# Row quantisation of the cross attention input: one of two VectorE passes replaced by a ScalarE pass, the lower clamp folded into ScalarE's Relu

## The reference

```
def fake_quant(x, scale, zp):
    q = jnp.clip(jnp.round(x / s + z), QMIN, QMAX)     # 0 and 255; z is 128
    return (q - z) * s
q1 = fake_quant(x1, x1_scale, x1_zp)
q2 = fake_quant(x2, x2_scale, x2_zp)
return jnp.matmul(q1, q2)
```

## Time and profile before

| what | value |
|---|---|
| median of 3 runs | 1863.63 us (1861.92 to 1865.05) |
| the profiled execution | 1863.91 us, its span in the trace 1862.1 us |
| PE busy | 1775.8 us (95%) |
| DVE busy | 1329.5 us (71%) |
| ACT busy | 970.2 us (52%) |
| POOL busy | 641.7 us (34%) |
| mean clock granted to PE | 0.992 |

### The profile page before, as it was taken

The page is one execution under the profiler, slowest core; times in us unless marked ns, Lnnn a source line. Parts: engine busy times, 40 slices in busy tenths (PEclk is TensorE's granted clock), DMA queues, the critical chain, the costliest instruction groups (busy, mean ns, idle before and its releaser), DMA issues.

```text
span 1862.1 us, 27416 instructions
## 1 busy us (share of the span) xinstructions
PE 1775.8 (95%) x9865; PEld 893.7 (48%) x9865; DVE 1329.5 (71%) x1867; ACT 970.2 (52%) x1432; POOL 641.7 (34%) x506
## 2 busy tenths in 40 slices
PE   6999999999999999999999999999999999999887
PEld 4454545444454545445454545445454545574333
DVE  7667776767677776767777766667677766659877
ACT  5555454645455454655454444555454444534674
POOL 2352334324342334324333333424333332301433
PEclk9999999999999999999999999999999999999998
DMA  4223224241423224241422214131322214133332
GB/s 172 84 69 108 69 90 108 72 105 46 136 63 108 69 91 108 69 107 46 136 63 69 74 57 108 57 85 46 98 67 68 75 57 108 57 106 122 114 91 91
DMA packets 158116, 161.52 MB, mean 87 GB/s; under 512 B 99872, under 2 KB 127904, under 8 KB 157600
## 3 DMA queue, kind: packets, MB, share of 16 engines
q1 hardware_dynamic: 146528, 147.09, 27.0%
q0 software_dynamic: 2560, 8.39, 1.4%
q10 hardware_dynamic: 8896, 4.28, 0.8%
HBM read 123.56 MB, written 12.58 MB: 73 GB/s over the span
## 4 chain that ended last, share of the span: by engine, by line
PE 67%; DVE 15%; issue 9%; ACT 7%; POOL 1%; DMA 1%; ACTq 0%; DVEq 0%; POOLq 0%
PE bank L1391 16%; PE bank L1393 16%; PE bank L1392 16%; PE bank L1364 4%; PE bank L1478 4%; PE bank L1480 4%; PE bank L1479 4%; DVE w_pair L1743 2%; DVE gated_split L1743 2%; DVE acc L1912 1%; DVE bank L1852 1%; PE bank L1542 1%; PE bank L1553 1%; DVE k_units L1892 1%; ACT L1632 1%
## 5 line engine op out<-in xcount | busy, mean ns | idle before, releaser
L1391 PE MATMUL bank<-x_blocks,w_pair 128*128 128x512 f16 (+1 forms) x1820 | 678.3, 373 | 34.4 <-ACT gate_units L1632 22.9
L1392 PE MATMUL bank<-x_blocks,w_pair 128*128 128x512 f16 (+1 forms) x1820 | 677.9, 372 | 0.0
L1393 PE MATMUL bank<-x_blocks,w_pair 128*128 128x512 f16 (+1 forms) x1820 | 677.9, 372 | 0.0
L1391 PEld LDWEIGHTS bank<-x_blocks,w_pair 128*128 128x128 f16 x1820 | 177.9, 98 | 241.2 <-ACT gate_units L1632 29.8
L2030 POOL TENSOR_TENSOR sums_pair<-raw_pair 128x512 f32<-128x512 f32 x63 | 92.4, 1467 | 563.8 <-DVE w_pair L1743 409.6
L1393 PEld LDWEIGHTS bank<-x_blocks,w_pair 128*128 128x128 f16 x1820 | 178.0, 98 | 202.8
L1392 PEld LDWEIGHTS bank<-x_blocks,w_pair 128*128 128x128 f16 x1820 | 178.1, 98 | 188.6
L1912 DVE TENSOR_TENSOR acc<-acc,bank 128x512 f32<-128x512 f32 x320 | 211.3, 681 | 20.8 <-PE bank L1480 20.5
L1641 ACT ACTIVATE bank<-bank 128x512 f32<-128x512 f32 x145 | 84.7, 584 | 211.1 <-PE bank L1393 210.9
L2056 POOL TENSOR_TENSOR ssq<-ssq,sig 128x512 f32<-128x512 f32 x64 | 81.8, 1278 | 283.8 <-ACT sig L1662 283.8
L1743 DVE SCALAR_TENSOR_TENSOR w_pair<-raw_pair,w_pair 128x1024 f16<-128x1024 f32 x126 | 158.8, 1270 | 21.2 <-ACT w_pair L1606 21.1
(11 more groups left out here) (216 smaller groups left out, 2677.4 us busy)
## 6 DMA issues: line engine op xcount, KB each, us to landing
raw_pair<-w_qk SPq DMA_DIRECT2D x32, 1024.0 KB, 5.5
raw_pair<-w_gate SPq DMA_DIRECT2D x16, 1024.0 KB, 4.9
raw_pair<-w_out SPq DMA_DIRECT2D x16, 1024.0 KB, 4.9
raw_pair<-w_vt SPq DMA_DIRECT2D x15, 1024.0 KB, 5.0
raw_pair<-ctx_in SPq DMA_DIRECT2D x8, 1024.0 KB, 4.9
decay_sb<-rates SPq DMA_DIRECT2D x60, 128.0 KB, 4.5
acc<-x_t SPq DMA_DIRECT2D x4, 1024.0 KB, 11.4
ctx<-raw_pair SPq DMA_DIRECT2D x8, 512.0 KB, 3.0
```

What stands on the lines that cost most here:

```text
L1391: pe.matmul(out, w_hi, x_hi, start=unmet and k == 0, stop=False, skip_group_check=halves or not fresh)
L1392: pe.matmul(out, w_hi, x_lo, start=False, stop=False, skip_group_check=halves or not fresh)
L1393: mm = pe.matmul(out, w_lo, x_hi, start=False, stop=k == QT - 1, skip_group_check=halves or not fresh)
```

## The change

`quantise` now takes three passes in another division. ACT's first pass uses Relu in place of Identity, so that the lower clamp to 0 is done by it. DVE makes one pass instead of two: minimum with 255, then plus the rounding constant, in place in fp32. A second, new ACT pass (Identity with scale 1 and a bias of minus the constant and minus 128, read from a one-column buffer `unround`) takes the constant off and writes the bf16 result. That pass waits for `q1_clamped`, for the constants, and for its destination to be free, and it is written directly behind the first one. DVE sets `unround` with one more small memset beside those of L1751 and L1752.

```
         self.ones32, self.neg_half = late[:, 0:P], late[:, P:P + ST]
+        self.unround = late[:, P + ST:P + ST + 1]
...
         elif kind == "quantise":
...
-            act.activation(c.raw[st["slot"]][:, :], c.acc[b][:, st["s"], :], ACT.Identity, bias=c.z1,
+            act.activation(c.raw[st["slot"]][:, :], c.acc[b][:, st["s"], :], ACT.Relu, bias=c.z1,
                            scale=c.inv1).then_inc(sem["q1_scaled"])
+            act.wait_ge(sem["constants"], 1)
+            act.wait_ge(sem["q1_clamped"], st["clamped"][1])
+            until(act, sem, st["dst_free"])
+            act.activation(c.q1_n[b][st["s"] % 2][:, :], c.raw[st["slot"]][:, :], ACT.Identity, bias=c.unround,
+                           scale=1.0).then_inc(sem["q1_n"])
...
             dve.memset(c.neg_half, -0.5)
+            dve.memset(c.unround, -(ROUND + Q_MID))
             dve.memset(c.ones32, 1.0).then_inc(sem["constants"])
...
         elif kind == "quantise":
             src = c.raw[st["slot"]][:, :]
             dve.wait_ge(sem["q1_scaled"], st["scaled"][1])
-            dve.tensor_scalar(src, src, 0.0, Q_MAX, ALU.max, ALU.min).then_inc(sem["q1_clamped"])
-            dve.wait_ge(sem["q1_clamped"], st["clamped"][1])
-            until(dve, sem, st["dst_free"])
-            dve.tensor_scalar(c.q1_n[b][st["s"] % 2][:, :], src, ROUND, ROUND + Q_MID, ALU.add,
-                              ALU.subtract).then_inc(sem["q1_n"])
+            dve.tensor_scalar(src, src, Q_MAX, ROUND, ALU.min, ALU.add).then_inc(sem["q1_clamped"])
```

## The result

The changed kernel takes **1869.51 us** (median of 6 runs, 1868.32 to 1870.93), the kernel before on the same chip 1863.53 (6 runs). The ratio is 1.0034, with a 95% interval of 1.0024 to 1.0045: 6.0 us more, where 6.4 were forecast. The profiled execution of the changed kernel took 1868.32 us, span 1866.3, and is the shortest of its six.

The account below looks back on a forecast made before the run. The prediction took DVE as full in the early tiles and PE as near full from 1760, with ACT's in-order queue deciding the cost. Tile terms summed to 6.40 us on the 1863.63 median, giving 1870.0 us, range 1865.5 to 1872.5.

Parts of the forecast that it names:

- T3: Third of eight row tiles: the square stands behind ACT's new pass, so DVE's gating comes later, +1.05 us.
- T5: Fifth row tile: two copies for batch 0's last store stand behind the new pass, delaying issue and first gather, +1.66 us.
- T7: Seventh row tile: Gelus and a split stand directly behind the new pass, and DVE's next split waits, +1.94 us.
- T6: Sixth row tile: up-weight split moves 1.94 us, covered by DVE's 1.80 us idle for POOL: 0, bounds -0.5 to +0.3.
- T1 and T2: First two row tiles: 0.44 us gained at first, then Silu late behind the new pass and DVE waits, +1.25 us.
- T4: Fourth row tile: quantised rows 0.44 us later for PE, less 0.38 slack before the store's transposes, +0.06 us.
- T8: Last row tile: PE, already waiting 0.68 us for the quantised rows, gets them 0.44 later, +0.44 us.
- The new pass: Added ACT pass of 128x1024 at each tile: 1.13 us, between 1.05 and 1.24, holding ACT for 1.04.
- rival (b): Half is taken up: 2.3 us of early delays hidden before the gather, 1867.7 us, or 1866.7; chance 0.20.
- Rival (a): Offload works: shifts behind the new pass fall into idle time, DVE's saving leaves 1.9 us less, 1861.7; chance 0.09.
- Rival (c): PE's clock stays low longer after longer waits at T3 and T5, costing another 1 to 3 us, 1871 to 1873; chance 0.11.

Follow-up runs that it names:

- T5 alone: The change's new form at the fifth row tile only, the old form at the other seven, against the kernel before: 1863.35 us, ratio 1.0008.
- T7 alone: The change's new form at the seventh row tile only, the old form at the other seven, against the kernel before: 1864.27 us, ratio 1.0013.
- saving alone: Against the kernel before: Relu in ACT's first pass, one DVE pass, no second ACT pass, upper clamp left out: 1863.71 us, ratio 0.9982.
- second trace of the changed kernel: The changed kernel run again, unaltered, on another chip: 1870.31 us against 1866.81 for the kernel before, ratio 1.0017.
- before again: The kernel before, unchanged, run and traced as if it were a changed one: 1862.76 us, ratio 1.0001.
- changed (second, third): Two repeats of the unaltered changed kernel on two other chips: 1870.31 us, ratio 1.0017, and 1870.67 us, ratio 1.0044, against the kernel before.
- T1/T4/T6/T8: The change's new form at these four row tiles only, the old form at the other four, against the kernel before: 1863.42 us, ratio 0.9985.
- wait alone: The kernel before plus ACT's wait for DVE's clamp after its first pass, no second ACT pass, both DVE passes kept: 1867.74 us, ratio 1.0007.
- pass twice: The changed kernel plus a third ACT pass per tile, copying the raw buffer onto itself before the new pass: 1877.16 us, ratio 1.0054.
- T2/T3/T5/T7: The change's new form at these four row tiles only, the old form at the other four, against the kernel before: 1870.09 us, ratio 1.0021.
- deferred: The changed kernel with the new ACT pass and its wait some steps later in ACT's queue at five tiles: 1862.89 us, ratio 0.9981.
- clamp in the copy: Against the kernel before: lower clamp in ACT's first pass, upper clamp in its existing transpose copy, one DVE pass, none added: 1864.39 us, ratio 0.9987.

## Why the prediction came true, step by step

The mechanism holds, and the largest terms (T3, T5 up to the store's issue, T7) came as worked out. That the sum is right within 0.3 us is in part luck: up to the issue of the store the shift is 0.64 less than my terms give, it loses 0.64 more ahead of T6's clamp, and the pass at T6 costs 0.92 where I had put 0.

| step | forecast | shift in the changed trace | by an experiment |
|---|---|---|---|
| T1 and T2 | +1.25 | +1.06 (-0.63 and +1.69) | +1.68 with T1 in the old form |
| T3 | +1.05 | +1.10 | +1.11 with T1, T4, T6, T8 in the old form |
| between T3 and the next gating | 0 | -0.30 | -0.31 with only T5 or only T7 changed |
| T4 | +0.06 | -0.15 | not apart |
| T5 | +1.66 | +1.67 | +1.67 alone up to the issue, 2.55 up to T8 |
| T6 | 0 | +0.27 (-0.64 and +0.92) | +0.07 with T2, T3, T5, T7 in the old form |
| T7 | +1.94 | +2.01 | +1.95 alone |
| T8 | +0.44 | +0.45 | +0.50 with T2, T3, T5, T7 in the old form |
| sum | 6.40 | 6.11 | |

**The new pass.** Taken at 1.13 us, measured 1.147. It held ACT for 1.05 us (1690.44 to 1691.49). The Trainium skill (ScalarE: Activation LUTs, What ACT_TABLE_LOAD costs) gave the same 1.13 as an estimate. The trace agrees within 0.02.

**T1 and T2: right in kind, 0.19 too high.** I let T1 gain 0.44, the wait of PE that the earlier trace rows shows. It gained 0.63. PE no longer waits for its sum there:

```profile
1684.85 1.46 PE L1365 MATMUL bank<-x_blocks,gated_split 128*128 128x512 f16 x6
```

The key split of T2 waited 2.76 where I had said about 2.7.

**T3: right.** The gating waits for the square, for 1.75 us where I had said 1.6. PE waits less than I thought, 3.05 and not some 4 us.

**T3 to T4: a gain that I did not have.** 0.30 go between T3 and the next gating, in the changed trace and in those of T5 alone and T7 alone. Why is not shown.

**T4: a sign I could not have read off.** I charged 0.06 for the late quantised rows. By the shift, DVE's gain was 0.15 larger than its wait for PE. Ahead of the store (1736.03) PE now waits for nothing, where it had waited 0.38.

**T5: right to 0.01.** First pass at R = 1742.07, copies at R + 3.09 (forecast 3.02). The first gather comes 4.26 later (forecast about 4), so rival (b) is out: the gap between T3 and T5 does not take the delay. It takes 0.45 of the shift (2.16 at T3's gating, 1.71 at T5's first pass), of which 0.30 also goes in traces in which nothing ahead had changed. The 4.26 is right by luck, though: my terms up to the issue of the store sum to 4.02, and the issue came at 3.38; the gather then came 5.40 us behind the issue where it had come 4.52, which I had left as it was. Why it takes longer is not shown.

```profile
1751.66 1.22 POOL L2076 DMA_INDIRECT acc<-x_t,perm_sb  x1 [10.04 <-issue]
```

**T6: the term that was mis-sized.** I took 0 with a bound of +0.3, and 0.27 came, but as the rest of two larger amounts. Between the issue and T6's clamp the shift falls from 3.38 to 2.74: DVE had waited 0.77 there. Behind the clamp it rises to 3.66, so the new pass costs 0.92 and is not covered. The 1.80 us of idle time were no fixed cover. POOL's instruction that is under way when DVE's split of the up weights ends always ends shortly behind it. In before that is the second gather, which takes 2.84 us where it takes 0.96 in the changed kernel; DVE's split and that gather:

```profile
1749.34 2.29 DVE L1743 SCALAR_TENSOR_TENSOR w_pair<-w_pair 128x2048 f16<-128x2048 f32 x1 [0.38 <-ACT w_pair L1719]
1749.62 2.84 POOL L2073 DMA_INDIRECT acc<-x_t,perm_sb  x1 [0.30 <-issue]
```

In the changed kernel both gathers are over in time, and it is the first of the power operations, with 1.95 us where it had 0.26:

```profile
1753.74 2.29 DVE L1749 SCALAR_TENSOR_TENSOR w_pair<-w_pair 128x2048 f16<-128x2048 f32 x1 [3.06 <-ACT w_pair L1725]
1754.17 1.95 POOL L2067 TENSOR_SCALAR scores_keys<-scores_keys 128x1 f32<-128x1 f32 x1
```

It is so in all fourteen traces: a gather ends 0.82 to 1.09 us behind the split, a power operation 0.08 or 0.09. DVE's idle time behind the split is therefore 1.80, 0.78 or 0.00 us by which of POOL's instructions it is, and it moves with the split. In the kernel with T5 alone it is the first gather, the idle time is 3.32, and that is where its shift grows from 0.66 to 2.18. That DVE's split holds POOL up is my reading of these times; no run varies it.

**T7 and T8: right.** From ACT's first pass to the next Gelu it takes 3.14 us where I had 3.07; PE waits 1.37 for T8's rows where it had waited 0.68, and 0.68 + 0.44 beyond it is 1.12, so PE itself came a little earlier:

```profile
1781.76 0.62 PE L1506 MATMUL bank<-ident,gate_units 128*128 128x128 bf16 x8 [1.37 <-ACT gate_units L1705]
```

**Rival (a)** was wrong in its condition, and its price was too small. The Trainium skill (Perfetto Trace Analysis, Optimizing Scalar/DVE Operations) says that with a saturated VectorE it may make sense to move work to ScalarE. Here that holds only with a better place in ACT's queue: written directly behind the first pass it costs 6.11 us at T8, some steps later T8 comes 0.30 earlier. As for the price, I had summed DVE's saving to 1.9; the trace of the saving alone gives 3.4. I had left out that the rows come 0.7 earlier at T8, where the earlier trace rows shows PE waiting for them, and the 0.3 behind T3.

**Rival (c)**, a lower PE clock behind the longer waits, did happen in the first trace and cost nothing up to T8. Behind T3's transposes the product took 5.96 us, where before, with a shorter low stretch, it took 4.68:

```profile
1709.49 5.96 PE L1522 MATMUL bank<-x_blocks 128*128 128x512 bf16 x16
```

In the second trace of the changed kernel the granted clock is 1.00 in the windows around T3 and T7 (in the first it is 0.83 and 0.86), that product takes 3.61 us, and the shift at T8 is 6.11 all the same:

```profile
1700.00:1720.00 20.00, 14.89 (x102) 7.72 (x100) 16.66 (x31) 10.37 (x14) 3.34 (x6) 1.00 0.75 250
...
1760.00:1780.00 20.00, 17.28 (x115) 6.60 (x112) 15.73 (x29) 17.42 (x26) 6.73 (x9) 1.00 0.25 67
```

PE is not the last there, so its slower pieces lie beside the others' work. My premise that the clock is low after such a wait does not hold either: in the second trace PE waits 3.05 us at T3, and its transposes then take 0.61 us, at full clock.

## What to carry to other kernels

In this kernel a pass moved to an engine with idle time cost nothing only at a place in that engine's queue where nothing urgent stands behind it: look there, and not at the busy share. Count the wait for the other engine apart from the pass, since it holds up the same work even if the pass were free. Where an operation fits into a pass that is made anyway (here a clamp as Relu in a scaling and in a copy), it took 3.9 us off the shift at T8, and the added pass put 6.1 on it. Shifts of single tiles cannot simply be added: where another engine is waited for, the same pass cost 0.07 or 0.92 us at T6.

## What the runs showed of the hardware that I had not expected

**Clock in the tail.** Behind T8 the shifts of the traces part again, by up to 4 us between the last sums of the two batches (PE, 1807.91 and 1840.74 in before). That goes with PE's granted clock in the 4 us windows at that piece of work. In the trace of before, of the changed kernel, and of before again:

```profile
1808.00:1812.00 4.00, 4.00 (x26) 2.76 (x28) 1.87 (x9) 0.45 (x1) 1.38 (x2) 0.67 0.59 179
1812.00:1816.00 4.00, 4.00 (x26) 1.61 (x24) 2.75 (x7) 3.44 (x8) 0.84 (x1) 0.90 0.00 0
```

```profile
1812.00:1816.00 4.00, 2.66 (x24) 2.27 (x26) 2.49 (x7) 0.63 (x1) 2.65 (x3) 1.00 0.69 193
1816.00:1820.00 4.00, 4.00 (x32) 1.69 (x26) 3.09 (x11) 3.96 (x8) 1.04 (x1) 1.00 0.24 70
```

```profile
1808.00:1812.00 4.00, 4.00 (x21) 2.27 (x20) 1.44 (x8) 0.94 (x2) 1.08 (x2) 0.51 0.44 125
1812.00:1816.00 4.00, 4.00 (x20) 2.26 (x18) 2.35 (x6) 2.21 (x6) 0.34 (x1) 0.63 0.00 0
```

The last column but two is the granted clock, and 0.50 of it is the lower level, 1.2 GHz. In the 4 us ahead of these windows it is 1.00 in all three, with PE busy for 1.92, 2.81 and 2.36 us of the 4. What the clock falls short of 1.00, summed over the 4 us windows from 1804 to 1828, goes with the distance between the two products:

| short of full clock, summed | traces | distance against before |
|---|---|---|
| 0 | changed (first), T1/T4/T6/T8 | -1.59, -1.44 us |
| 0.42, 0.43 | before; changed (second, third), wait alone, pass twice, T2/T3/T5/T7 | -0.03 to +0.04 |
| 0.85, 0.86 | before again, deferred, T5 alone, T7 alone | +1.58 to +1.62 |
| 1.28 | saving alone, clamp in the copy | +2.63, +2.75 |

A difference of 0.43 of the full clock over 4 us is 1.7 us of matmuls at full clock, which is about what a step of the table shows. In the last row the low stretch begins about 1.1 us ahead of the first of the two products, so a part of it lies outside the distance. The same program has it one way or the other from one execution to the next (before and before again differ by 1.58 us in it), so a single trace says nothing on a change of 2 us at the end of the kernel. Why PE gets one or the other is not shown by any run.

**The kernel before differs by chip, the changed one does not.** Its median was 1863.5, 1866.3, 1866.8 and 1862.4 us in the four groups of runs, the changed kernel's 1869.5, 1870.3 and 1870.7. Why it was 3 to 4 us slower in two groups stays open: no trace of it was taken there, and the clock in the tail is a candidate only. The mean granted clock of each run is on record, and it does not explain it: the runs of the kernel before at 0.992 have medians of 1866.2 and 1866.4 us in the two groups and 1862.8 in the last. How much of the advantage that the deferred pass, the clamp in the copy and the four light tiles had there would show on another chip is therefore open too; by the traces it is 0.30, 3.88 and 1.26 us up to T8, the last with 0.74 of clock in it.

**Three prices of one ScalarE pass.** At 128x1024 it takes 1.06 us with a number as scale and no bias buffer, 1.15 with a bias buffer, and 1.24 (median) with both from buffers. So each such buffer costs about 0.09 us, even one of a single column.
